# Two attention layers on one core: the rows of units 1 to 3 through HBM and VectorE's transpose

## The reference

```python
xn = group_norm(x, gamma, beta)              # 32 groups of 8 channels, over all tokens of the image
q = conv1x1(xn, wq, bq); k = conv1x1(xn, wk, bk); v = conv1x1(xn, wv, bv)
scores = jnp.einsum('bnc,bmc->bnm', q, k) * C ** -0.5
attn = jax.nn.softmax(scores, axis=-1)
out = jnp.einsum('bnm,bmc->bnc', attn, v)
y = conv1x1(out, wp, bp) + x
```

## Time and profile before

| | us |
|---|---|
| Median of three runs (264.43 to 264.79) | 264.69 |
| The profiled execution | 264.73 |
| its span | 262.6 |
| PE busy | 254.3 (97%) |
| DVE busy | 187.5 (71%) |
| ACT busy | 153.3 (58%) |
| POOL busy | 124.2 (47%) |

### The profile page before, as it was taken

The page is one execution under the profiler, slowest core; times in us unless marked ns, Lnnn a source line. Parts: engine busy times, 40 slices in busy tenths (PEclk is TensorE's granted clock), DMA queues, the critical chain, the costliest instruction groups (busy, mean ns, idle before and its releaser), DMA issues.

```text
span 262.6 us, 4590 instructions
## 1 busy us (share of the span) xinstructions
PE 254.3 (97%) x1614; PEld 228.2 (87%) x1614; DVE 187.5 (71%) x473; ACT 153.3 (58%) x299; POOL 124.2 (47%) x143
## 2 busy tenths in 40 slices
PE   7999999999999999999989999999999999999985
PEld 6787789889998899789987899789987899889985
DVE  0589977886983797679776698679776688549703
ACT  3656544699984519645667509746486509740920
POOL 2010801285769209517475907717274917800860
PEclk9999999999999999999999999999999999999999
DMA  6960000000000000000000000000110001100102
GB/s 201 347 217 0 0 1 2 0 0 2 0 4 0 0 2 1 0 2 1 0 1 2 0 2 0 0 2 0 41 41 3 0 2 40 40 2 19 50 14 80
DMA packets 6989, 7.37 MB, mean 28 GB/s; under 512 B 556, under 2 KB 6712, under 8 KB 6968
## 3 DMA queue, kind: packets, MB, share of 16 engines
q1 hardware_dynamic: 6944, 7.08, 8.1%
q10 hardware_dynamic: 24, 0.01, 0.0%
HBM read 4.99 MB, written 2.10 MB: 27 GB/s over the span
## 4 chain that ended last, share of the span: by engine, by line
PE 60%; DVE 21%; ACT 8%; issue 6%; POOL 4%; POOLq 0%; DVEq 0%; ACTq 0%
PE ring L1027 11%; PE ring L1029 10%; PE ring L1028 10%; PE ring L1066 5%; PE ring L1068 4%; PE ring L1067 4%; DVE S L729 4%; POOL P_lo L312 3%; ACT P_hi L456 3%; DVE xnat L739 2%; PE ring L1013 2%; ACT S L457 2%; PE ring L1014 2%; PE ring L1015 2%; PE Z L914 2%
## 5 line engine op out<-in xcount | busy, mean ns | idle before, releaser
L312 POOL TENSOR_TENSOR P_lo<-S,P_hi 128x512 fp32r<-128x512 f32 x64 | 81.9, 1302 | 73.7 <-ACT S L457 73.5
L1066 PE MATMUL ring<-V,P_hi 128*128 128x258 f32 x256 | 72.9, 285 | 0.9 <-POOL P_lo L312 0.9
L1068 PE MATMUL ring<-V,P_lo 128*128 128x258 f32 x256 | 72.2, 282 | 0.0
L1067 PE MATMUL ring<-V,P_hi 128*128 128x256 f32 x256 | 72.2, 282 | 0.0
L456 ACT ACTIVATE P_hi<-S 128x512 fp32r<-128x512 f32 x64 | 40.2, 628 | 43.0 <-DVE S L729 43.0
L449 ACT COPY S<-ring 128x512 f32<-128x512 f32 x64 | 37.2, 589 | 37.9 <-PE ring L1029 36.2
L1027 PE MATMUL ring<-t_hi,xn_lo 128*128 128x512 f32 x128 | 51.8, 405 | 0.0
L1029 PE MATMUL ring<-t_hi,xn_hi 128*128 128x512 f32 x128 | 50.0, 391 | 0.0
L1028 PE MATMUL ring<-t_lo,xn_hi 128*128 128x512 f32 x128 | 50.0, 391 | 0.0
L1066 PEld LDWEIGHTS ring<-V,P_hi 128*128 128x128 f32 x256 | 48.4, 189 | 1.6 <-POOL P_lo L312 1.1
L1067 PEld LDWEIGHTS ring<-V,P_hi 128*128 128x128 f32 x256 | 48.4, 189 | 0.5
(11 more groups left out here) (116 smaller groups left out, 355.4 us busy)
## 6 DMA issues: line engine op xcount, KB each, us to landing
xnat<-in_x SPq DMA_DIRECT2D x8, 256.0 KB, 6.9
out<-xnat SPq DMA_DIRECT2D x16, 128.0 KB, 1.7
wide<-in_vectors SPq DMA_DIRECT2D x2, 384.0 KB, 7.6
w_wq<-in_L_conv_wq SPq DMA_DIRECT2D x2, 256.0 KB, 4.8
w_wk<-in_L_conv_wk SPq DMA_DIRECT2D x2, 256.0 KB, 5.0
w_wv<-in_L_conv_wv SPq DMA_DIRECT2D x2, 256.0 KB, 6.9
w_wp<-in_L_conv_wp SPq DMA_DIRECT2D x1, 256.0 KB, 6.6
w_wp<-in_L_conv_wo SPq DMA_DIRECT2D x1, 256.0 KB, 7.5
```

What stands on the lines that cost most here:

```text
L312: nc.gpsimd.tensor_tensor(P_lo[:, exp_of(c, kb), :], S[:, tile_of(c, kb), :], P_hi[:, exp_of(c, kb), :].bitcast(F32), ALU.subtract).then_i ...
L1066: nc.tensor.matmul(bank[:, 0:C + 2], P_hi[:, tile, mine], v[:, kb, 0:C + 2], start=(kb == 0), stop=False)
L1067: nc.tensor.matmul(bank[:, 0:C], P_hi[:, tile, mine], v[:, kb, C + 2:VX], start=False, stop=False)
L1068: last = nc.tensor.matmul(bank[:, 0:C + 2], P_lo[:, tile, mine], v[:, kb, 0:C + 2], start=False, stop=(kb == NB - 1))
```

## The change

- The rows of units 1 to 3 no longer pass PE and ACT. They are loaded a second time from HBM into a new buffer `moved`, in pieces of 32 channels of one token (128 bytes), so that block a of 32 partitions holds 32 tokens with the channels of quarter a side by side. DVE transposes the 32x32 blocks from `moved` to `xraw` at the head of `statistics_of`.
- For unit 1 the source is the input x: eight DMAs for the whole image, queued on SP ahead of the second image; all four turns wait for all of them. For units 2 and 3 the source is a new HBM buffer `between`, into which SP stores each 128 rows of layer 0's output behind DVE's `output`. Two quarters are loaded together and then one and one.
- `next_rows` and ACT's `raw_rows` for units 1 to 3 are gone. POOL's `residual` waits for the load or the store instead of for PE's transposes.
- In units 1 and 2 the statistics for the next unit stand behind running maxima 4 and 7 of `first` (3 and 6 before), and behind 4 and 7 of `second` (around the outputs before). Both group products stand inside the second query tile of the attention of `first`; `variance` and `affine_map` inside `maxima_to_all(second)`. ACT normalises all four quarters, t_high of the next unit stands behind four pairs of exponentials instead of two, and DVE's t_low behind the outputs. PE's product for the next unit's first half of t follows the fourth query tile instead of the second.
- `maxima_to_all` keeps intermediates in X (PSUM) instead of `other` (SBUF).
- The last chunk goes by keys for five key tiles (`BY_KEYS`).

```diff
+            def load_moved(v, r, n=1):
+                source = x[v] if v < IMAGES else between[v - IMAGES]
+                pieces = source.rearrange("(t j) (k a c) -> k a j t c", j=SQ, k=KC, c=SQ)
+                place = moved[:, :, :, :, :].rearrange("p k i g c -> p k (i g) c")
+                tokens = slice(2 * QUARTERS * r, 2 * QUARTERS * (r + n))
+                for k in range(KC):
+                    for a in range(QUARTERS):
+                        sp.dma_start(place[a * SQ:(a + 1) * SQ, k, tokens, :], pieces[k, a, :, tokens, :]
+                                     ).then_inc(mv_x[v, r], 16)
+            load_moved(1, 0, NR)
             load_image(1)
+            for b in range(IMAGES):
+                for r, n in ((0, 2), (2, 1), (3, 1)):
+                    for i in range(2 * r, 2 * (r + n)):
+                        sp.wait_ge(dv_O, b * NB + i + 1)
+                        sp.dma_start(between[b, i * P:(i + 1) * P, :], xnat[:, b, i, :]).then_inc(st_x[b][i // 2], 16)
+                    sp.wait_ge(dv_turn, b * NR + r + n)
+                    for s in range(r, r + n):
+                        sp.wait_ge(st_x[b][s], 32)
+                    load_moved(IMAGES + b, r, n)
...
             def statistics_of(v, r):
-                dve.wait_ge(ac_xT, v * NR + r + 1)
+                if v == 0:
+                    dve.wait_ge(ac_xT, r + 1)
+                else:
+                    if v > 1:
+                        wait_for_x_low(dve, v - 1, TQ)
+                    dve.wait_ge(mv_x[v, 0 if v == 1 or r == 1 else r], MOVED)
+                    nc.vector.transpose(xraw[:, :, 2 * r * P:2 * (r + 1) * P],
+                                        moved[:, :, 2 * r:2 * r + 2].rearrange("p k i g c -> p k (i g c)")
+                                        ).then_inc(dv_turn, 1)
+                    dve.wait_ge(dv_turn, (v - 1) * NR + r + 1)
...
-            def attention(c, before_third, before_last):
+            def attention(c, behind, statistics=False):
                 pe.wait_ge(po_P, (c + 1) * NB)
                 for j in range(QB):
                     wait_for_bank("O", c, j)
                     for kb in range(NB):
                         attend(c, j, kb)
-                    if j == 1:
-                        before_third()
-                    if j == 2:
-                        before_last()
+                        if statistics and (j, kb) == (1, 2):
+                            mean_of_groups(c // 2 + 1)
+                        if statistics and (j, kb) == (1, 6):
+                            variance_of_groups(c // 2 + 1)
+                    if j in behind:
+                        behind[j]()
...
             for kb in range(NB):
                 scores(0, kb)
-                if kb < NR:
-                    next_rows(1, kb)
                 if kb == 6:
                     mean_of_groups(1)
...
-            for kb in range(NB // 2):
+            for kb in range(BY_KEYS):
                 attention_by_keys(CHUNKS - 1, kb)
```

More of the change, by code:

```diff
@@ L85, in two_attention_layers @@
         if u < UNITS - 1:
[L86 removed]
+            ring_order += [("O", 2 * u, j) for j in range(QB)]
             ring_order += [("t", u + 1, 0, k) for k in range(KC)]
[L88 removed]
         else:
@@ L498, in _ @@
                     score_copy(first, kb)
-                    if more and kb in (3, 6):
-                        raw_rows(u + 1, kb // 3 - 1, Z)
                 for kb in range(NB):
@@ L504, in _ @@
                         t_high(u, 1, kb - 3)
-                    if more and kb == 6:
-                        raw_rows(u + 1, 2, Z)
                     exponentials(first, kb)
@@ L510, in _ @@
                     score_copy(second, kb)
-                    if kb == 0 and more:
-                        raw_rows(u + 1, 3, Z)
                 if more:
-                    for q in range(KC):
-                        xn_high(u + 1, q)
-                    for q in range(KC, TQ):
+                    for q in range(TQ):
                         normalise(u + 1, q)
-                    for q in range(KC, TQ):
-                        xn_high(u + 1, q)
+                        if q:
+                            xn_high(u + 1, q - 1)
+                    xn_high(u + 1, TQ - 1)
                 for kb in range(6):
-                    if more and kb in (2, 3):
-                        t_high(u + 1, 0, kb - 2)
+                    if more and kb in (4, 5):
+                        t_high(u + 1, 0, kb - 4)
                     exponentials(second, kb)
@@ L803, in _ @@
                     running_max(first, kb)
-                    if more and kb in (3, 6):
+                    if more and kb in (4, 7):
                         statistics_of(u + 1, kb // 3 - 1)
@@ L818, in _, with statistics_again @@
                 output(before, 2)
+                output(before, 3)
+                def statistics_again():
+                    if more:
+                        variance(u + 1)
+                        affine_map(u + 1)
+                for kb in range(1, 5):
+                    running_max(second, kb)
                 if more:
                     statistics_of(u + 1, 2)
-                output(before, 3)
+                running_max(second, 5)
+                running_max(second, 6)
+                running_max(second, 7)
                 if more:
@@ L860, in _ @@
                     output(first, 3)
+                    t_low(u + 1, 0, 0)
+                    t_low(u + 1, 0, 1)
                 else:
@@ L1162, in _ @@
             for j in range(QB):
-                for kb in range(NB // 2, NB):
+                for kb in range(BY_KEYS, NB):
                     attend(CHUNKS - 1, j, kb)
```

112 lines of the change are left out of this document (40 added, 72 removed).

## The result

| | before | after |
|---|---|---|
| median of seven runs each, side by side, us | 264.64 (264.43 to 264.87) | 266.06 (265.57 to 267.15) |
| ratio, 95% interval | | 1.0060 (1.0044 to 1.0077) |
| profiled execution, us | 264.73 | 266.42 |
| its span, us | 262.6 | 264.7 |

The change makes the kernel 1.4 us slower. The prediction was 266.7, slower. The total was met, but no part of its sum was: one cost was left out, two were too high, and the gain at the end was too small. These errors nearly cancel. A few executions of the experiments took far longer than the rest (356.84 to 1387.12 us); the ratios and intervals leave them out.

The account below looks back on a forecast made before the run. TensorE (PE), busy for 97% of the span, was taken as the bound as long as its feeders keep up. 264.73 + 2.15 (stage 1) + 0.70 (entries) - 0.87 (end) = 266.7 us, range 265.0 to 271.0.

Parts of the forecast that it names:

- Transposes off PE: Twelve sets of four transposes leave PE, 5.2 us of its work; whether that arrives at the end asked stage by stage.
- The turn: DVE's 128x512 transpose from SBUF to SBUF ahead of the statistics: 0.73 us, 0.76 with the wait of its reader.
- Stage 1, the aggregates: Scores of unit 0: four DVE rounds take 8.8 us, PE waits 3.8 at unit 1's group means, costing 2.15.
- The clock: Rival, chance 0.07: PE's clock falls to 1.2 GHz in stage 1's 3.8 us wait, some 2 us more, 268.7.
- the prediction's own sign of being wrong: Wrong if the wait at the group mean is under 1 us, or if the granted clock drops.
- The load of unit 1: 128-byte pieces at some 20 ns each land near 25 us, before DVE wants them at 31.04: nothing to pay.
- Loads of units 2 and 3: Through HBM behind DVE's outputs; the last quarter's rows ready near 106.7, ten microseconds for store and load: no cost.
- Stage 2: Unit 1's first half to its second: second scores start at 104.3, 0.9 us earlier, though DVE's chain moves 0.7 later.
- Entries: Starts of units 2 and 3: ACT is waited for, first value copy 136.2 for 135.81; 0.35 us each, 0.7 in all.
- The end: Last attention: a fifth key tile puts 12 products, 1.43 us, into PE's wait for POOL of 0.87: minus 0.87 us.

Follow-up runs that it names:

- f6_last_quarter_late: Changed kernel with unit 1's fourth turn, statistics and aggregates behind chunk 0's shift, group-mean products behind score tiles of chunk 1: 263.93 us, ratio 0.9973.

## Why the prediction was right, and where not

| term | predicted | measured |
|---|---|---|
| start of the first scores | 0 | -0.22 |
| stage 1, DVE's aggregates late | +2.15 | +1.62 |
| stage 1, the clock behind the wait | 0 (a rival at +2) | +1.51 |
| all between the scores of chunk 1 and the last attention | +0.70 | -0.47 |
| the end | -0.87 | -1.13 |
| sum | +1.98 | +1.31 |

- *Transposes off PE, 5.2 us.* Right that they bring nothing by themselves where DVE or ACT is waited for. They do bring something in stage 2, see below.
- *The turn.* 0.701 us as the group of its 12 instructions has it, 0.73 to the reader behind it, against 0.73 and 0.76: right, and the nearer bound was the right one to lean on. It costs the same into SBUF as into PSUM, to within 0.03.
- *Stage 1, the aggregates.* The mechanism, the place, the wait (3.56 against 3.8) and the releaser are right; the size was 0.53 too high, counted from the first scores. The term that was mis-sized is the round: 2.20 predicted, 2.00 measured. I took 0.84 for a pair of statistics from the earlier trace rows, which had a small gap in it; in the tighter order it takes 0.67, and the turn took 0.03 less. The four rounds took 8.10 instead of 8.80, and they began 0.21 sooner with the first scores, so the aggregates start at 38.33 instead of 39.24; 0.17 is given back by their length and the step to PE.
- *The clock.* This was a rival, at 0.07 and priced at 2 us, and it belonged in the forecast. It came in every execution of the kernel after (mean clock 0.987 to 0.994), and the filled wait shows that it is worth 1.46 to 1.51. A dropping clock is also the prediction's own sign of being wrong, and that sign came true. Its price was estimated well, its chance not: the waits of the kernel before were of 1.1 us or less (PE has one of 1.1 near the start, which the prediction overlooked), and I read that as no evidence rather than as a sign that nothing here had been tried. The Trainium skill (TensorE: Matmul & The Clock Gate, Part 1) says that the clock depends on how busy the engine has been of late; the trace agrees, with 0.50 granted from 40 to 42 us.
- *The load of unit 1.* Right that it is hidden; 20 ns a piece was too much, 13.7 is what the doubled load shows. It had landed by 25.3 with the image behind it.
- *Loads of units 2 and 3.* No wait for them, as forecast. The last quarter's loads were issued from 111.07 to 114.84 and turned at 119.30.
- *Stage 2.* Predicted: second scores 0.9 sooner relative to the first. Measured: 106.81 - 2.87 = 103.94 against 105.19, so 1.25 sooner. The last maximum is 0.95 sooner instead of 0.72, and turn and statistics take 1.41 instead of 1.51.
- *Entries.* The order of events was right throughout: PE idle 1.07 before t (1.5 predicted), ACT without a gap from the normalisation, the value copies late. But each time was 0.36 to 0.45 too late, the shift 123.44 for 123.8, the exponentials 128.35 for 128.8, the first value copy 135.75 for 136.2. This is the 0.35 of stage 2 carried on, and it happens to be the cost that I put on an entry. Two of the sums there do not come out as written: 119.2 + 12 x 0.119 is 120.6 and not 120.85, which decides nothing since DVE reads the variance later, and 2 x 1.52 + 2 x 1.04 is 5.1 and not 4.95, where the trace has 4.91. So 0.35 became -0.05 in unit 2. In unit 3 it was -0.30, and the last 0.08 came behind it.
- *The end.* The mechanism was right, and -0.87 was read from the idle time; read from the starts of the products it would have been 1.14, as shown above. The kernel before with this edit alone gains 0.41%.

The forecast of 266.7 stands 0.6 from the measured 266.06. Had every term but the clock been sized rightly, it would have been 264.73 + 1.62 - 0.47 - 1.13 = 264.75, no change: the clock is what makes the kernel slower, and with the wait filled it is level with before. By its stated reason (DVE's turns make PE wait in stage 1) the prediction was right, in that this wait causes all of the 3.13, 1.62 by itself and 1.51 by the clock behind it. That the sum came out within 0.6 is luck: it was helped by errors of opposite sign.

**What beats both kernels** is the change for units 2 and 3 with PE's transposes kept for unit 1 and the variances read sooner: 260.79 us, ratio 0.9833.

## What to carry to other kernels

Work moved from the busiest engine to its feeder pays only where the feeder had slack at that place. Here the same edit costs 3.1 us in the first unit, where VectorE is already late, and gives 0.5 back in the others, where its new work lies beside long attentions; ask stage by stage, and apply it to the stages that have room. A new wait of 2 to 4 us on TensorE, as here, should be priced as the wait plus 1.5 us for the products behind it at half the clock, with a chance of its own (half of the executions behind 2.03 us, nearly all behind 3.56), and filling it with products that nobody reads is a cheap way to find out. Read what a wait costs from the starts of the instructions around it, not from the idle time beside it.

## What was unexpected of the hardware

- Behind an idle stretch of 3.56 us TensorE ran at 1.2 GHz from 39.5 to 42.9 in the profile; the mean clock was below 1 in all seven executions of after, in all seven with the doubled load, and in five of six with four key tiles. Behind an idle stretch of 2.03 us it was so in six of twelve; behind the waits of 1.1 us the profiles show 1.00. A fall cost 1.4 to 1.5 us.
- 128-byte pieces from HBM to SBUF ran at 150 GB/s, 13.7 ns a piece on each of 16 engines, and SyncE's time to issue eight DMAs of 1024 pieces was 10.75 and 11.52 us while earlier loads still ran at 310 to 400 GB/s until 14.5, and 6.14 behind those.
- A float32 transpose of 128x512 in 32x32 blocks on VectorE, SBUF to SBUF, takes 0.70 us, against 0.73 into PSUM.
- VectorE steps of 0.15 to 0.17 us took 0.93 to 1.25 us in two places where GpSimd was at work beside them: the maxima's intermediates in the kernel before (120.48 and 121.45), and r0sq and r_err at 49.59 and 50.87 in f6_last_quarter_late.
